# Resident expert stages: next stage's weight loads issued behind the fifth tile's store instead of ahead of the first

## The reference

```python
def _moe_group(x2, router_w, wg, wu, wd, top_k):      # layer 2
    scores = jax.nn.softmax(x2 @ router_w, axis=-1)
    expert_weights, expert_indices = lax.top_k(scores, top_k)
    ...
    ys = lax.ragged_dot(jax.nn.silu(gate) * up, wd, group_sizes)
    ys = ys * flat_w[order][:, None]
    return jnp.zeros_like(x2).at[tok].add(ys)
...
h = jax.nn.silu(g) * u                                # layer 0, I = 352
expert_out = jnp.einsum('nei,ehi->neh', h, experts_down)
out = jnp.einsum('neh,ne->nh', expert_out, w) + shared_weight * shared
```

## Time and profile before

| | us |
|---|---|
| median of 3 runs | 2392.01 (2388.96 to 2405.95) |
| profiled execution, time of its own | 2405.93 |
| its span (first to last instruction) | 2404.2 |
| "experts0", SP's first issue to last store issued | 160.7 to 338.8 |
| "experts2_0", the same | 1701.3 to 1817.0 |
| "experts2_1", PE's first work to last store issued | 1855.6 to 1990.7 |

### The profile page before, as it was taken

One profiled execution on the slowest core, in us unless ns is written; L12 is line 12 of the kernel. 1 busy time (PEld: TensorE's weight loads), 2 busy tenths in 40 slices (PEclk: granted clock), 3 DMA queues, 4 the chain that ended last, 5 costly groups with the idle time before them and its releaser, 6 DMA issues. The chain is left out here.

```text
span 2404.2 us, 41453 instructions
## 1 busy us (share of the span) xinstructions
PE 1978.3 (82%) x13179; PEld 1597.3 (66%) x13201; DVE 1261.0 (52%) x4235; ACT 916.6 (38%) x2192; POOL 776.0 (32%) x1055
## 2 busy tenths in 40 slices
PE   6849999986899999999579966885693896797594
PEld 5737766664889988988579954554582675454594
DVE  2542225543788888887400046674435345785423
ACT  3623222423233333333323335554442343575321
POOL 1012211101354444453111052310454646441132
PEclk9959999987999999999789988996796998899697
DMA  3232221001411011100199752436477475433294
GB/s 139 102 120 62 60 86 37 18 14 35 49 32 27 24 33 32 28 15 1 43 336 346 271 154 58 101 66 246 147 150 246 139 140 150 85 94 118 74 332 147
DMA packets 173308, 261.88 MB, mean 109 GB/s; under 512 B 23088, under 2 KB 138800, under 8 KB 169008
## 3 DMA queue, kind: packets, MB, share of 16 engines
q1 hardware_dynamic: 153040, 212.45, 27.8%
q0 software_dynamic: 16704, 45.64, 8.3%
q10 hardware_dynamic: 3360, 1.18, 0.4%
HBM read 181.19 MB, written 37.75 MB: 91 GB/s over the span
## 5 line engine op out<-in xcount | busy, mean ns | idle before, releaser
L2190 PE MATMUL heads_ps_c<-heads_band,heads_sT 128*128 128x129 f32 x3072 | 368.8, 276 | 13.4 <-DVE heads_band L2415 12.3
L2190 PEld LDWEIGHTS heads_ps_c<-heads_band,heads_sT 128*128 128x128 f32 x3072 | 354.9, 192 | 23.7 <-issue 21.7
L508 POOL DMA_INDIRECT weights_xg<-xn_rows,token_of x197 | 191.3, 971 | 453.1 <-DVE token_of L694 176.4
L2353 POOL TENSOR_SCALAR heads_band<-heads_shifts,heads_taps 128x130 f32<-128x130 f32 x384 | 253.4, 674 | 242.1 <-PE heads_ps_c L2190 238.4
L2283 ACT ACTIVATE heads_probs<-heads_mixes,heads_least 128x256 f32<-128x256 f32 x256 | 116.1, 500 | 342.3 <-DVE heads_least L2428 342.3
L2415 DVE SCALAR_TENSOR_TENSOR heads_band<-heads_shifts,heads_taps,heads_band 128x130 f32<-128x130 f32 x768 | 226.7, 351 | 18.9 <-POOL heads_band L2353 14.3
L1870 ACT ACTIVATE heads_probsT<-heads_ps_e 128x512 f32<-128x512 f32 x256 | 148.0, 597 | 102.4 <-PE heads_ps_e L1719 91.4
L1041 PE MATMUL experts_ps_g<-weights_w,experts_xT 128*128 x504 | 136.7, 395 | 5.0 <-ACT experts_xT L1091 2.7
L1064 PE MATMUL experts_ps_y<-weights_w,experts_hT 128*128 (+1 forms) x486 | 134.9, 386 | 2.1 <-DVE experts_y L1126 1.1
L1695 PE MATMUL heads_ps_m<-heads_stackK,heads_stackQ 96*128 96x256 bf16 x512 | 99.8, 281 | 28.5 <-DVE heads_negmax L1920 21.0
L1719 PE MATMUL heads_ps_e<-heads_stackQ,heads_stackK 99*128 99x256 bf16 x512 | 101.1, 281 | 22.6 <-ACT heads_probsT L1870 19.7
(11 more groups left out here) (409 smaller groups left out, 4215.6 us busy)
## 6 DMA issues: line engine op xcount, KB each, us to landing
experts_w<-in_experts_dram SPq DMA_DIRECT2D x23, 2180.0 KB
weights_w<-in_experts_dram SPq DMA_DIRECT2D x16, 1536.0 KB
weights_w<-in_experts_dram SPq DMA_DIRECT2D x32, 768.0 KB
y_rows<-experts_y SPq DMA_DIRECT2D x125, 128.0 KB
heads_stackK<-heads_k_pieces SPq DMA_DIRECT2D x192, 64.0 KB
heads_stackQ<-heads_q_pieces SPq DMA_DIRECT2D x192, 64.0 KB, 2.5
weights_w<-in_experts_dram SPq DMA_DIRECT2D x8, 1088.0 KB
xn_rows<-xn SPq DMA_DIRECT2D x4, 2048.0 KB, 7.5
```

Source lines behind the costliest of these rows:

```text
L508: pool.indirect_dma_start(self.xg[:, u, :], None, xn_dram, bass.IndirectOffsetOnAxis(ap=tb.token_of[:, j:j + 1], axis=0)).then_inc(self.x_ ...
L2190: last = pe.matmul(out[:, qc * SEQ + k0:qc * SEQ + k1], sT[:, h % 2, kc, qc * P + dq:qc * P + dq + P], band[:, h % 2, dq, w0:w0 + k1 - k0] ...
L2353: last = pool.tensor_scalar(band[:, h % 2, dq, :], shifts[:, 0, :], taps[:, r % 2, h, dq * TAPS:dq * TAPS + 1], None, ALU.mult)
```

## The change

SP issues the first five stores of the stage, then the loads, then the other stores. Nothing else is altered; the stage without a prefetch keeps its order.

```diff
+    FIRST_TILES = 4
...
         def _(sp):
-            if prefetch is not None:
-                prefetch(sp)
             for j in range(NT):
                 sp.wait_ge(y_copied, j + 1)
                 sp.dma_start(y_dram[j * P:(j + 1) * P, :], y[:, j % YB, :]).then_inc(stored[j % YB], 16)
+                if prefetch is not None and j == FIRST_TILES:
+                    prefetch(sp)
```

## The result

| | before | changed |
|---|---|---|
| median, us (20 runs each) | 2399.25 (2388.96 to 2405.95) | 2405.9 (2396.6 to 2415.11) |
| profiled execution, its span | 2405.93, 2404.2 | 2415.11, 2413.4 |

The ratio is 1.0031, interval 1.0019 to 1.0042: the change costs 7.4 us, 4.6 to 10.1. Forecast were 1.6 us less. So the sign was wrong. The size lies within 1%, where I had put 0.96 of the chance, but the time, 2405.9, is outside my range of 2381 to 2399. Of the 15.5 us between 2390.4 and that time 7.2 are the base, 2392.01 from three runs, which became 2399.25 over 20 and so lies above the range by itself; the other 8.3 are the change.

A forecast was written before the change was run, and what follows sets the result against it. PE, busy 82% of the span, was taken to bound the kernel, through its work and waits. -5.09 - 4.05 + 5.5 + 2.0 = -1.6 us from the median 2392.01 gave 2390.4 us, range 2381 to 2399.

The forecast's parts named there:

- Part 1, "experts0": Start of "experts0": PE's wait for tile 1's gathered rows falls from 8.33 to 3.24 us, 5.09 us less.
- one of my signs of being wrong: Listed sign of error: a difference in stages that the change doesn't touch; no size given.
- Part 1, "experts2_0": Start of "experts2_0": tile 1's wait falls from 7.29 to 3.24 us, 4.05 us less, with nothing late next.
- Part 4: "experts2_0" after PE's stall: the clock drops to half for some 4.1 us of PE's time, 2.0 us lost.
- Part 2: Moved loads in "experts0": done before `copy_out(9)` needs store 5, 21 us after `copy_out(4)`; cost 0.
- Part 3: Middle of "experts2_0": store 5 waits behind the loads in SP's queue, `copy_out(9)` is late, PE loses 5.5 us.
- my slow end: "experts2_0": loads take the old 15.88 us, store 5 done at T0 + 17.4, 9.7 us late; PE loses 8.3.
- My rival "the start is not freed": Tile 1 still comes 7 us after its gather, so no gain: +7.5 us, 2399.5 us; chance 0.10.

The follow-up runs named there:

- after_ahead4: The changed kernel with 4 instead of 8 tiles gathered ahead in "experts2_0" and "experts2_1"; ratio to the kernel before 1.0011.
- only0_ahead4: The changed kernel with "experts2_0" loads back at its start and 4 instead of 8 tiles gathered ahead in "experts2_0" and "experts2_1"; ratio to the kernel before 0.9973.
- actq: The changed kernel with the two loads of "experts2_0" issued from ScalarE's queue instead of SP's; ratio to the kernel before 1.0001.
- spread: The changed kernel with the two loads of "experts2_0" cut into eight of 384 KB, one behind each second store from the fifth; ratio to the kernel before 0.9995.
- Burst_mid: As spread, but in "experts2_0" and "experts2_1" POOL gathers 4 tiles ahead until tile 24, then up to 8; ratio to the kernel before 1.0008.
- only0: The changed kernel with only the loads of "experts0" moved, those of "experts2_0" at its start; ratio to the kernel before 0.9948, repeated 1.0007.
- Only2: The changed kernel with only the loads of "experts2_0" moved, those of "experts0" at its start; ratio to the kernel before 1.0027.

## Why the prediction was wrong

- **Part 1, "experts0"** (-5.09). The stage itself became 5.84 us shorter. The shared stage behind it became 2.78 longer. Both appear only together: where "experts0" has moved loads the sum is 402.1 to 402.7 in twelve of the thirteen profiles of the table (404.4 in the other), however it is shared out. Timeline of PE at the shared stage's start, before and after:

```profile
341.73 2.05 PE L2590 MATMUL shared_ps_g<-xnT,layer_shared_w 128*128 128x256 f32 x4 [3.71 <-PEq L69]
...
346.64 7.03 PE L2610 MATMUL shared_ps_a<-layer_shared_hist,layer_shared_ctx 128*128 128x512 f32 x16
```

```profile
334.01 2.04 PE L2591 MATMUL shared_ps_g<-xnT,layer_shared_w 128*128 128x256 f32 x4 [3.71 <-PEq L69]
335.85 1.91 PE L2591 MATMUL shared_ps_u<-xnT,layer_shared_w 128*128 128x256 f32 x4
...
340.35 7.03 PE L2611 MATMUL shared_ps_a<-layer_shared_hist,layer_shared_ctx 128*128 128x512 f32 x16
```

  The first 16 matmuls take 6.34 us instead of 4.91. Four of them took 1.91 us here and 1.03 later in the trace before. That is the lower clock, held longer: 1.43 of the 2.78 us. Most of the rest is the same once more, 80 us into the stage. PE, first before, then after:

```profile
421.24 1.13 PE L2590 MATMUL shared_ps_g<-xnT,layer_shared_w 128*128 128x256 f32 x4
```

```profile
415.03 2.08 PE L2591 MATMUL shared_ps_g<-xnT,layer_shared_w 128*128 128x256 f32 x4
416.90 1.68 PE L2591 MATMUL shared_ps_u<-xnT,layer_shared_w 128*128 128x256 f32 x4
```

  The next sixteen matmuls of this kind take 5.11 us instead of 3.56: the granted clock was 0.50 over 415 to 417, where the trace before had 1.00 throughout. After a part of it is regained, 1.2 us remain. So one of my signs of being wrong came true, a difference in a stage that the change does not touch, and it is a term that I had left out: how much of a gain the next stage gives back at the lower clock. Net -3.1.
- **Part 1, "experts2_0"** (-4.05). This is the step that failed. I wrote "nothing is late next" after a look at rows' arrival alone. Behind PE's wait stood a second limit: POOL's eleven gathers in a row, under which ScalarE and DVE, and by them PE, run late until 14 to 15 us behind the table load. The old trace showed it in "experts2_1", whose tile 1 came 3.24 us after its gather and whose first store was no earlier (16.3 us against 14.1). Its timeline:

```profile
1864.23 1.03 PE L1041 MATMUL experts_ps_g<-weights_w,experts_xT 128*128 x4
...
1868.97 0.28 ACT L1098 ACTIVATE experts_silu<-experts_ps_g 128x128 f32<-128x128 f32 x1 [4.16 <-DMA xn<-y_rows,slot_of]
...
1869.63 0.33 PE L1056 MATMUL experts_ps_h<-ident,experts_h 128*128 128x128 f32 x1 [2.61 <-issue]
```

  The silu on tile 2 starts 3.7 us after its matmuls end, and PE's 2.61 us behind it are the very "wait of 2.6 us at 1867" from which Part 4 read the clock, without asking what PE had waited for. That "PE is never idle" once a stage runs was shown for the stretch of the earlier trace rows only. I took three starts as evidence and followed each only to PE's first matmul, not to the first store. Measured +0.8 at `copy_out(0)` where -4.05 was forecast, the largest part of the miss (4.9 of 9.9 us). In after_ahead4 and only0_ahead4, with the burst short, the term is real: 4.0 us (9.5 against 13.5).
- **Part 2** (0). Right: "experts0" has no new wait for a store, and `copy_out(9)` comes 21.1 us after `copy_out(4)`, as before.
- **Part 3** (+5.5). The mechanism was right, its place too: `copy_out(9)`, five tiles after `copy_out(4)`. I chose the middle of three paces for the loads. With T0 the issue of the fifth store (the last of the five that end at 1708.81 + 7.29, so 1715.8), `copy_out(9)` began at T0 + 17.1, my slow end (T0 + 17.4): from their issue at 1716.13 to their last packet at 1731.97 the loads took 15.8 us, as in the earlier trace rows. I had given them 402 GB/s once PE and POOL stood still; all queues together moved 296 to 360, gathers that were left over and first stores among it. PE lost 7.40, not 5.5. By the trace the store waits for the load DMA engine by DMA engine: of the packets in 1726 to 1728 17 were under 2 KB, as a store's are and a load's are not, in 1728 to 1730 361, while the last packets of the loads still moved. The Trainium skill's page "DMA: Bandwidth & Descriptors", section "Queues, rings and completion order", states that each DMA engine consumes what stands in one queue in order. The trace agrees, and so does actq, with the loads in another queue: 1.9 us.
- **Part 4** (+2.0). The clock was 0.50 from about 1729 to 1739 and PE worked 5.6 us of that (1733.53 to 1739.2): about 2.8 us. It dropped once, as forecast.
- **The sum again**: -3.1 + 0.8 (copy_out(0)) + 0.6 (to copy_out(4), which takes 6.97 us instead of 6.33: the granted clock fell to 0.61 and 0.53 over 1708 to 1712, behind PE's late spots) + 10.2 (7.4 and 2.8) = +8.5, with 8.3 in the table of stages. My rival "the start is not freed" had +7.5 and a chance of 0.10. Its number was nearly met, but not by its mechanism: tile 1 did come early.

The Trainium skill's page "Runtime: NRT & Kernel Launch", section "Instruction fetch mechanics", has a rule that would explain ScalarE's lateness otherwise: a taken branch to a page of instructions that the engine does not hold makes it fetch that page by DMA before it goes on, and a stage opens with a branch. The trace does not bear it out. In the stretch 1704 to 1712 of spread, in which ScalarE stands, the queues moved only gathers, and no packet of the instruction queue:

```profile
DMA packets 282, 0.76 MB, mean 95 GB/s; under 512 B 96, under 2 KB 96, under 8 KB 282
## 3 DMA queue, kind: packets, MB, share of 16 engines
q0 software_dynamic: 282, 0.76, 37.3%
```

Burst_mid has the same lateness far from any branch at a stage's start. Its first late spot (1734 to 1736) has no packet of the instruction queue either, its second (1736 to 1739.3) has one.

**What stays open.** By what means POOL's back-to-back gathers hold ScalarE's instructions up (and DVE's and PE's, whose rows read "issue" there) is not shown. Nor is why the clock fell once more 80 us into the shared stage, nor why only0 was timed 12 us under the kernel before once and level with it the next time. Only2's stages show +15 us and its timing +6.5, which I can't reconcile except by that scatter.

## What to carry to other kernels

Before a bulk load is moved down a queue, count who waits behind it: the slack of the next store (here five tiles of 1.63 us) has to exceed the load at its slowest pace, with what else moves; if not, cut it small (with 384 KB behind every second store no store was awaited for more than 1.4 us, as before the change) or use another queue. A wait that is removed at a stage's start is a gain only once the first output has moved as well: compare the first store's distance in a stage that never had the wait. And a deep gather-ahead is not free: here the three stages from "experts2_0" on took 286.8 and 283.6 us with 5 tiles ahead, 293.0 with 8.

## What the runs showed of the hardware

Gathers that POOL issues without a pause, 0.95 us each and 1.25 us apart, go with late work on ScalarE and DVE: instructions whose inputs are ready start up to 5.4 us later (`copy_rows(4)` in "experts2_1" of spread: ready at 12.5 us behind the table load, started at 17.9). By what means is open. Eleven in a row (thirteen in "experts2_1") put the first store of a stage at 14 to 18 us, five (four tiles ahead) at 8.8 to 10.1 where no load stood in the way, plain loads of the same rows from SP at 8.2. Six in a row in mid-stage left ScalarE idle for 1.6 and 2.5 us. A store behind 3.15 MB in SP's queue made DVE wait 9.34, 9.84 and 8.09 us in three kernels. With the loads in ScalarE's queue it was 1.94 at most.
